# A four-layer network in one launch: the third layer's token gathers are issued three stages earlier, and its buffers are zeroed by two repeated-source transfers

## The reference

```python
    def _L2_ffn_ref(x, gate, W1, b1, W2, b2, Ws1, bs1, Ws2, bs2):
...
        scores, token_idx = jax.lax.top_k(flat_probs, k=capacity)
...
        tok = flat_x[token_idx]
        h = jax.nn.gelu(jnp.einsum('ecd,edh->ech', tok, W1) + b1[:, None, :])
        out_tok = jnp.einsum('ech,ehd->ecd', h, W2) + b2[:, None, :]
        scaled = out_tok * scores[..., None]
        routed = jnp.zeros_like(flat_x).at[token_idx.reshape(-1)].add(scaled.reshape(E * capacity, D)).reshape(G, S, D)
        shared = jax.nn.gelu(jnp.einsum('gsd,dh->gsh', x, Ws1) + bs1)
        shared = jnp.einsum('gsh,hd->gsd', shared, Ws2) + bs2
        return routed + shared
```

## Time and profile before

| | |
|---|---|
| median of 3 timed runs | 2531.06 us (2530.04 to 2534.03) |
| profiled execution | 2541.07 us |
| its span in the trace | 2539.3 us, so 1.8 us lie around the span |
| TensorE busy | 1930.7 us (76%) |
| VectorE busy | 1431.9 us (56%) |
| ScalarE busy | 914.7 us (36%) |
| GpSimd busy | 318.3 us (13%) |

### The profile page before, as it was taken

How to read it: one execution, slowest core, us unless ns; L and a number is a source line. 1 busy time by engine, 2 the same in 40 slices (tenths; PEclk the granted TensorE clock), 3 DMA queues, 4 the chain that set the end, 5 groups by cost and what they waited for, 6 DMA issues and landing times.

```text
span 2539.3 us, 34708 instructions
## 1 busy us (share of the span) xinstructions
PE 1930.7 (76%) x11846; PEld 1311.0 (52%) x11846; DVE 1431.9 (56%) x5329; ACT 914.7 (36%) x2089; POOL 318.3 (13%) x455
## 2 busy tenths in 40 slices
PE   6687566666666595995989866799997755698887
PEld 5455356555555454784545654555453344493333
DVE  2656688888888825576133345454121123348985
ACT  2332233333333312332234311345443321455766
POOL 0000100000000000131000000200031614414642
PEclk8788755655556567897789955699998976797989
DMA  2000200000000000000000110000020330353662
GB/s 98 1 6 11 43 17 22 17 22 17 17 22 17 6 30 0 2 3 1 1 0 1 67 36 0 1 1 1 1 96 15 28 105 27 76 89 60 107 96 41
DMA packets 89503, 76.05 MB, mean 30 GB/s; under 512 B 22384, under 2 KB 80624, under 8 KB 88432
## 3 DMA queue, kind: packets, MB, share of 16 engines
q1 hardware_dynamic: 81648, 65.31, 11.3%
q0 software_dynamic: 7680, 8.53, 1.8%
HBM read 48.86 MB, written 23.51 MB: 29 GB/s over the span
## 4 chain that ended last, share of the span: by engine, by line
PE 45%; DVE 26%; issue 5%; DMA 4%; SPq 2%; ACT 2%; POOL 2%; another core or an unknown queue 1%; ACTq 0%; DVEq 0%; POOLq 0%
PE ps L204 41%; DVE sm L225 7%; DVE mw L225 4%; DMA d_pt<-big 2%; PE ps L208 2%; DVE big L225 2%; DVE big L217 2%; PE ps L2230 1%; SPq L2317 1%; POOL d_acc L1992 1%; DVE sm L217 1%; DVE big L231 1%; DVE sm L231 1%; DVE sm L221 1%
## 5 line engine op out<-in xcount | busy, mean ns | idle before, releaser
L204 PE MATMUL ps<-ke,big 32*128 32x128 f32 (+2 forms) x1632 | 206.5, 325 | 135.6 <-DVE big L225 135.1
L213 ACT ACTIVATE sm<-sm 128x1 f32<-128x1 f32 x512 | 174.5, 341 | 354.9 <-DVE sm L225 222.3
L204 PEld LDWEIGHTS ps<-ke,big 32*128 32x128 f32 (+2 forms) x1632 | 172.7, 222 | 179.3 <-DVE big L225 166.1
L204 PE MATMUL ps<-big,mw 128*128 128x512 f32 (+3 forms) x476 | 238.2, 598 | 18.2 <-ACTq L252 12.9
L213 ACT ACTIVATE tmp<-ps,bi 128x512 f32<-128x512 f32 (+1 forms) x226 | 153.6, 683 | 215.8 <-PE ps L204 184.3
L213 ACT ACTIVATE big<-ps,co 128x512 f32<-128x512 f32 (+1 forms) x296 | 176.6, 646 | 65.0 <-PE ps L204 64.2
L231 DVE TENSOR_REDUCE big<-ps 128x2 f32<-128x512 f32 x256 | 162.4, 677 | 26.5 <-PE ps L204 26.2
L204 PE MATMUL ps<-big,tmp 128*32 128x256 f32 (+1 forms) x1148 | 132.3, 423 | 54.0 <-DVE tmp L221 28.9
L204 PE MATMUL ps<-ke 48*128 48x256 bf16 (+4 forms) x638 | 142.5, 345 | 38.8 <-DVE big L217 17.5
L204 PE MATMUL ps<-tmp,mw 128*128 128x512 f32 (+1 forms) x320 | 157.7, 604 | 1.3 <-ACT tmp L212 1.3
L204 PE MATMUL ps<-big 128*32 128x128 f32 (+6 forms) x930 | 150.9, 320 | 9.6 <-DMA big<-big 3.2
(11 more groups left out here) (246 smaller groups left out, 3796.4 us busy)
## 6 DMA issues: line engine op xcount, KB each, us to landing
mw<-d_tab SPq DMA_DIRECT2D x32, 328.0 KB, 3.5
mw<-m SPq DMA_DIRECT2D x2, 4096.0 KB, 12.4
d_pt<-big SPq DMA_DIRECT2D x32, 192.0 KB
ke<-d_pt SPq DMA_DIRECT2D x72, 64.0 KB
big<-d_pt SPq DMA_DIRECT2D x72, 64.0 KB
mw<-d_pt SPq DMA_DIRECT2D x48, 64.0 KB
d_xs<-big SPq DMA_DIRECT2D x5, 512.0 KB
big<-d_xs SPq DMA_DIRECT2D x5, 512.0 KB, 6.3
```

The lines of the kernel that those rows point to most:

```text
L204: return e.matmul(out, lhsT, rhs, start=start, stop=stop)
L213: return e.activation(out, in_, f, bias=K("zero")[0:out.shape[0], :] if bias is None else bias, scale=scale, **kw)
```

## The change

Four edits. `zeros` moves from 1024 columns of `BIG[7]` to 256 columns of `BIG[3]`, behind the space of the gathers, and is repeated as the source of the zeroing: one transfer of 16 repeats for `d_acc` and one of 20 for `d_xs`. The memset moves on VectorE from the start of stage 29 to the start of stage 26. GpSimd waits for stage 25 in place of stage 28 before the gathers of experts 0 to 6. Before the four gathers of expert 7, whose place in `BIG[7]` is in use until stage 27, it waits for stage 28.

```diff
-        zeros = BIG[7][:, 1024:2048]
+        zeros = BIG[3][:, 3840:4096]
+
+        def blank(r):
+            return zeros.rearrange("p (r n) -> p r n", r=1).broadcast_to((128, r, 256))
...
         def fetch_sp(e):
             e.wait_ge(*ex_z(1))
-            for q in range(4):
-                e.dma_start(d_acc.rearrange("(p b) d -> p (b d)", p=128)[:, 1024 * q:1024 * q + 1024], zeros).then_inc(s_z, 16)
-            for q in range(5):
-                e.dma_start(d_xs.rearrange("(p b) d -> p (b d)", p=128)[:, 1024 * q:1024 * q + 1024], zeros).then_inc(s_zx, 16)
+            e.dma_start(d_acc.rearrange("(p b) d -> p (b d)", p=128).rearrange("p (r n) -> p r n", n=256), blank(16)).then_inc(s_z, 16)
+            e.dma_start(d_xs.rearrange("(p b) d -> p (b d)", p=128).rearrange("p (r n) -> p r n", n=256), blank(20)).then_inc(s_zx, 16)
...
             for c in range(32):
+                if c == 28:
+                    e.wait_ge(stage_end, 3 * 28)
                 e.indirect_dma_start(gx(c // 4)[:, 136 * (c % 4):136 * (c % 4) + 136], None, d_xt,
                                      bass.IndirectOffsetOnAxis(ap=IX[:, c:c + 1], axis=0)).then_inc(s_g[c // 4], 16)
...
-            e.wait_ge(s_z, 64)
+            e.wait_ge(s_z, 16)
...
-            e.wait_ge(s_zx, 80)
+            e.wait_ge(s_zx, 16)
...
             barrier(e, st.up())
+            fetch_dve(e)
             ln_dve(e, LNB)
...
             barrier(e, st.up())
-            fetch_dve(e)
             ffn_dve(e, 16, 16, B("bs2"), X1_, X1_, H1)
...
             places_pool(e, gn)
-            e.wait_ge(stage_end, 3 * 28)
+            e.wait_ge(stage_end, 3 * 25)
             fetch_pool(e)
```

## The result

| | before | after |
|---|---|---|
| median of 20 timed runs each | 2533.29 us (2523.57 to 2542.2) | 2552.53 us (2540.13 to 2565.37) |
| ratio of after to before | | 1.0069, 95% interval 1.0054 to 1.0085 |
| profiled execution | 2541.07 us | 2543.17 us, span 2541.4 us |

The change costs 17.5 us (0.0069 x 2533.29) to 19.2 us (the medians). Gain was forecast, 2528.3 us in a range of 2512 to 2535.

A forecast was written before the change was run, and what follows sets the result against it. The prediction took TensorE and VectorE to bound the kernel (71% of the span). Removing one stall (-17.2 us) and adding one in `LNB` (+14.4) gave -2.8 on 2531.06, so 2528.3 us, in a range of 2512 to 2535.

The forecast's parts named there:

- The stall that is removed: Shared feed-forward: without gathers beside it, it takes its twin's time plus one VectorE addition, 17.2 us saved.
- The twin feed-forward: The feed-forward two stages before the shared one, 58.65 us with as many matmuls, taken as the time without a stall.
- The memset, the zeroing, the other waits: `LNB`'s start, the zeroing's transfers and GpSimd's waits: all covered by other waiting, nothing gained or lost.
- The stall that is added: `LNB`: the moved run of gathers stalls it for 17.4 to 20.8 us, losing 11.5 to 17.3, taken as 14.4 us.
- the second case: Queries, keys and values stage: stall beside the scatter into `d_xs`, read as beginning 21.6 us after the first scatter.
- a share of the time: `LNB`: part of the stall's length that is lost, 0.66 or 0.83 from the two stalls of before.
- the stall doesn't come back: Rival: no stall in `LNB`, so -17.2 us, 2513.9, or 2518.5 if part belongs to tracing; chance 0.28.
- the gathers aren't the cause: Rival: the shared feed-forward's stall has another cause, so moving the gathers gives nothing, 2531 us; chance 0.12.
- The stall begins sooner and it gets slower: Rival: in `LNB` the stall starts before 1775 to 1780, making the kernel slower, 2534 to 2541 us; chance 0.15.
- Its worst case: `LNB`: the stall begins with the gathers, 39.5 us long, 26.1 us lost, so +8.9 us: 2540.
- The chances: Whole kernel: stall moves along 0.45, doesn't come back 0.28, another cause 0.12, sooner and longer 0.15.

The follow-up runs named there:

- The cut kernel: The kernel before with the shared feed-forward's first matmuls (128 x 512) issued as four of 128 columns: ratios 1.0030, 1.0006, 1.0049, on chips without stalls.
- the groups of four and eight: GpSimd waits for each group's landing: gathers in fours, scatter in eights against before, 0.9845; gathers in fours in the changed kernel, 0.9900 to before; stalling chip.

## Why the prediction was wrong, by its own steps

**The stall that is removed: right.** 17.2 us reckoned, 17.8 measured. The twin feed-forward was a good measure of it.

**The memset, the zeroing, the other waits: right.** The memset took 0.27 us (0.3 reckoned). The first gather started 1.3 us after `LNB`'s first matmul (1.4 reckoned), the 28th 33.9 us later (33.9). The zeroing alone gave a ratio of 1.0003 on the chip without stalls, and without it the stall in `LNB` was there on the other (26.11 against 27.49 us). The trace counts 3,344 more packets than before; 4608 less 1152, or 3,456, were reckoned.

**The stall that is added: the failed step.** That it would come, and end 5 to 6 us after the run's last start, was right (5.65). Its size was 11.5 to 17.3 us by the prediction, and `LNB` lost 31.0. Three things in the term were wrong.

*When it begins.* The prediction counted microseconds or gathers from the run's start, and it read the second case late. It took VectorE's wait of 10.52 us in the queries' stage for the first. ScalarE had begun a long wait there 3.6 us earlier, at 2143.10, and VectorE's 4.30 us before its row at 2145.96 were long already. ScalarE in order of time, before:

```profile
2142.41 0.69 ACT L213 ACTIVATE big<-ps,bi 128x512 f32<-128x512 f32 x1 [0.41 <-PE ps L204]
2148.06 0.69 ACT L213 ACTIVATE big<-ps,bi 128x512 f32<-128x512 f32 x1 [4.96 <-remote]
```

So both cases began at 18 to 19 us. Counted in TensorE's matmuls these and `LNB` fit better than in microseconds. From the first transfer to ScalarE's first wait of over 3 us, the shared feed-forward of before had 44 matmuls in 18.99 us, the queries' stage 49 in 18.10, and `LNB` of the changed kernel 42 in 12.59:

```profile
1879.53:1898.52 18.99, 18.99 (x44) 8.29 (x43) 2.89 (x4) 9.42 (x13) 14.42 (x16) 0.95 0.80 300
...
2125.00:2143.10 18.10, 12.57 (x49) 7.58 (x50) 7.29 (x10) 5.50 (x8) 14.09 (x14) 0.75 0.14 48
```

```profile
1749.61:1762.20 12.59, 11.63 (x42) 7.40 (x41) 4.00 (x9) 4.69 (x7) 9.65 (x10) 0.64 1.02 344
```

These are before's trace and the changed kernel's. On the other stalling chip `LNB` had 48 and 49 matmuls in 12.1 and 13.4 us, and the queries' stage, in the changed kernel's trace and three from that chip, 50 to 52 in 18.1 to 19.6 us. In all nine stalls that is 42 to 52 matmuls and 12.1 to 19.6 us. Smaller delays came before some of these waits: in `LNB` of the changed kernel ScalarE got a result at 1759.52 after 2.28 us, where the tile of before that is its like had it 1.1 us sooner after its last matmul's start. Undisturbed, `LNB` issues 144 in 30.96 us (4.7 a microsecond) and the shared feed-forward 128 in 58.65 (2.2), so `LNB` gets there sooner.

*What is lost in it.* The prediction carried over a share of the time. The rows of the stalls show something nearer to a rate, in stages whose matmuls have 128 and 512 columns and in one where they have 1, 128 and 512:

```profile
1898.52:1924.46 25.94, 12.95 (x23) 4.69 (x21) 1.44 (x2) 2.06 (x4) 16.06 (x17) 0.77 0.18 48
2146.65:2170.49 23.84, 10.82 (x26) 5.09 (x24) 0.69 (x2) 2.75 (x4) 15.12 (x16) 0.67 0.14 47
```

That is 0.89 and 1.09 matmuls a microsecond in before, 0.96 (26 in 26.97) in the changed kernel, and 20 in 27.49 (0.73) and 20 in 26.11 (0.77) in the two `LNB`s on the other chip. The queries' stage from ScalarE's first long wait on, 2143.10, had 40 in 27.39 us (1.46), since TensorE went on for a while with matmuls that waited for nothing. So the figure is a mean over bursts and pauses, from 0.7 to 1.5, and depends on where a stretch is cut. A stage that needs 4.7 a microsecond loses 1 - 0.96/4.7 = 0.80 of such a stretch, one that needs 2.2 loses 0.6. The 26 matmuls take 5.6 us in `LNB` undisturbed, so 21.4 us are lost in the stall.

*The clock, which was not in the sum.* The last 76 matmuls took 21.10 us at a granted 0.58; before's last 93 took 17.07 us at 0.85, which is 13.9 us for 76, so 7.2 us are lost after the stall is over. The early gathers alone, on the other chip, lie between the two: the last 76 in 18.27 us at 0.69.

```profile
1799.06:1817.33 18.27, 14.37 (x76) 12.24 (x77) 7.54 (x19) 7.96 (x15) 0.00 (x0) 0.69 0.01 1
```

The first 43 took 13.89 us at 0.62, where before had 53 in as long: 2.6 us, of which 1.1 are the result that came late at 1759.52. After the idle 0.96 us that followed, eight matmuls of 128 columns took 1.71 us (at 1760.27), while their like in before took 1.13. With 21.4 that makes 31.2, and 31.0 were measured; the parts are cut from one trace, so the sum shows where the time lies and tests nothing.

That the clock follows the idle time is read from rows, not tried. That the stall counts matmuls is argued from nine stalls in three stages, of which only `LNB` begins at another time than the others, and was not shown by an experiment. Results that are waited for fit less evenly: 5 for 16 matmuls in the shared feed-forward and 3 for 18 in `LNB` give 3.6 and 6.2 us for each, where a matmul comes to 1.13 and 1.04 us. On the other chip `LNB` gives 1.37 and 1.31 us for a matmul and some 8 us for a result. The cut kernel on a stalling chip would tell.

**The rivals.** That the stall doesn't come back is refuted for chips that stall, and describes the others. That the gathers aren't the cause falls with the groups of four and eight: each stall goes, or nearly, when the run beside it is broken up, and stays where the run is left whole. The Trainium skill (SBUF — State Buffer, "SBUF: two separate sides") says that engines and transfers reach SBUF by different ports and can't slow each other. For the traffic itself the runs agree: in the changed kernel with gathers in fours, on the chip without stalls, TensorE is busy 10.00 of 10.00 us in `LNB` beside 346 GB/s. As a reason to expect no harm from transfers it does not hold where stalls exist. *The stall begins sooner and it gets slower* is what happened, with 0.15 given to it, and its sign was seen: waits in `LNB` from 13.9 us after its start, where 14.9 (1775) was the limit. Its mechanism (sooner, since `LNB` signals more densely) had the right direction. Its worst case, 26.1 us, fell short of 31.0 for the same reason as the main one: the share of 0.66, and no clock.

**The chances** had a gap besides: all evidence came from one chip's trace, and no case said that the stall might not exist on another. There the change is worth nothing either way (the early gathers alone 0.9983, with 1 in the interval; the whole change was not run there).

## What to carry to other kernels

Where GpSimd would issue dozens of indirect transfers in a row beside TensorE work, make it wait after every fourth for the group to land. Where there was no stall such waits cost nothing that could be told from the spread of the measurements (0.9978 for the gathers in fours, 1.0034 and 0.9995 with the scatter in fours too). Where there was one, gathers in fours and the scatter in eights took 36.7 us off 2532.22, in runs that were all recorded. Before such a run is moved, count TensorE's matmuls in its new surroundings beside the microseconds (the better guide in nine stalls, though not tested), and ask what the clock does after the gap. And run the kernel before on a second chip, and if possible without recording, before a stall is taken for a property of the kernel.

## What the runs showed of the hardware that was not expected

- The stall differs from chip to chip, or from one set of timings to another: only one chip was used twice, without a stall both times. Where the change was timed, and on one more chip, before took 2533.29 and 2532.22 us. On three others it took 2493.62, 2489.43 and 2486.27 us, and none of the fourteen traces from there has a stall under a long run.
- In a stall TensorE gets through 0.7 to 1.5 matmuls a microsecond on average, in bursts with pauses of up to 14 us. ScalarE's first wait of over 3 us begins 42 to 52 matmuls after the run's first transfer, and the last late result comes 4.5 to 5.9 us after its last.
- A layer norm of many small matmuls leaves the stall at a granted clock of 0.58 and stays there for 21 us, to its end; the feed-forward after it has 0.96 again, over its 58.58 us.

What holds TensorE back is open. One candidate is the recording itself. Every timed run came with a record of its span and granted clock, as the profiled one did, so whether a run without any recording stalls is not shown. The late results, the like cost for matmuls of any size and the beginning after some fifty of them would fit a path for records that fills up, and so would the releasers that the trace can't name in the stalls. The Trainium skill (NOTIFIC — the notification-queue block, "7.1 Overflow: three behaviours, one of which stalls the engine") says that the block which writes trace records holds back its producers when its internal buffers fill, rather than lose a record. No run here shows whether that happened, and it would not by itself say why GpSimd's transfers set it off or why only on some chips. If it is so, both the loss of 17.5 to 19.2 us and the gain of 36.7 us belong to recorded runs.
